# Where a graph-transformer layer fills a scratch tensor, and which engines take a maximum over partitions

## The reference, cut to what matters

```
xn = layernorm(x)
x  = x + gnn(xn, edges) + mix(xn)          # mix: attention with random features, 16 heads of 64
x  = x + ffn(layernorm(x))                 # 8 experts, the two best of each row, softmax of their logits
# gnn: h = xn @ W.T + b; out = segment_sum(deg^-1/2[row] * deg^-1/2[col] * h[col], row)
# mix: q, k, v = xn @ W.T + b; phi = exp(x @ orf.T - |x|^2/2) + eps; out = phi(q) @ (phi(k).T @ v) / (phi(q) @ sum phi(k))
# ffn: out = sum over the two experts e of score_e * (x @ expert_w[e] + expert_b[e])
```

## Time and profile before

| | value |
|---|---|
| median of three runs | 1686.0 us |
| profiled execution, its own time | 1684.43 us |
| its span, first to last instruction | 1682.3 us |
| mean granted TensorE clock, share of full | 0.954 |
| TensorE matmul / VectorE / ScalarE / GpSimd busy | 88% / 44% / 26% / 20% |
| DMA traffic over the span | 150.64 MB |

### The profile page before, as it was taken

One profiled execution on the slowest core, in us unless ns is written; L12 is line 12 of the kernel. 1 busy time (PEld: TensorE's weight loads), 2 busy tenths in 40 slices (PEclk: granted clock), 3 DMA queues, 4 the chain that ended last, 5 costly groups with the idle time before them and its releaser, 6 DMA issues.

```text
span 1682.3 us, 25130 instructions
## 1 busy us (share of the span) xinstructions
PE 1477.8 (88%) x7987; PEld 1219.1 (72%) x8051; DVE 747.2 (44%) x1413; ACT 436.9 (26%) x727; POOL 343.4 (20%) x333
## 2 busy tenths in 40 slices
PE   4718788899998999999999999998999589999990
PEld 1406667664446999999999999997788578888870
DVE  6805555412002454544544444444545514554436
ACT  6300111111001333332333232333213202332320
POOL 5510212112310111010110101000413311212233
PEclk9959999999999999999999999999999679999995
DMA  3580001141211000000000000000432515566648
GB/s 144 190 287 10 22 5 35 35 144 63 94 63 35 26 23 19 21 25 12 25 12 25 25 12 25 0 1 19 127 125 95 200 56 206 194 237 246 234 167 298
DMA packets 54830, 150.64 MB, mean 90 GB/s; under 512 B 7130, under 2 KB 14250, under 8 KB 54480
## 3 DMA queue, kind: packets, MB, share of 16 engines
q1 hardware_dynamic: 48096, 127.20, 21.5%
q0 software_dynamic: 6688, 22.83, 4.3%
HBM read 119.72 MB, written 48.64 MB: 100 GB/s over the span
## 4 chain that ended last, share of the span: by engine, by line
PE 82%; DVE 5%; issue 4%; another core or an unknown queue 2%; DMA 2%; ACT 2%; POOL 2%; DVEq 1%; POOLq 0%; SPq 0%; ACTq 0%
PE PB L1406 10%; PE PB L1435 7%; PE PB L1437 7%; PE PB L1436 7%; PE PB L1611 5%; PE PB L1612 5%; PE PB L1614 5%; PE PB L1471 4%; PE PB L1494 4%; PE PB L1356 4%; PE PB L1394 2%; PE PB L1417 2%; PE PB L1395 2%; PE PB L1396 2%
## 5 line engine op out<-in xcount | busy, mean ns | idle before, releaser
L1435 PE MATMUL PB<-xh,hw 128*128 128x416 f32 (+1 forms) x576 | 206.0, 358 | 4.9 <-POOL orfl L692 4.9
L1437 PE MATMUL PB<-xh,hw 128*128 128x416 f32 (+1 forms) x576 | 204.1, 354 | 0.0
L1436 PE MATMUL PB<-xl,hw 128*128 128x416 f32 (+1 forms) x576 | 203.9, 354 | 0.0
L1406 PE MATMUL PB<-h,AT 128*128 128x512 f32 x400 | 171.9, 592 | 1.2 <-ACT h L835 1.2
L1611 PE MATMUL PB<-mwh,mth 128*128 128x512 f32 x368 | 149.0, 405 | 1.3 <-issue 1.3
L1406 PEld LDWEIGHTS PB<-h,AT 128*128 128x128 f32 x400 | 75.9, 190 | 96.5 <-issue 94.6
L1612 PE MATMUL PB<-mwl,mth 128*128 128x512 f32 x368 | 144.6, 393 | 0.0
L1356 PE MATMUL PB<-ohs,ohd 128*128 x471 | 103.6, 342 | 42.4 <-DVE ohs L1031 29.1
L1394 PE MATMUL PB<-wqh,xh 128*128 128x256 f32 x320 | 93.5, 292 | 41.6 <-ACT h L829 39.9
L1029 DVE TENSOR_SCALAR ohd<-iota,dc 128x128 f16 x178 | 69.1, 388 | 134.0 <-PE PB L1356 122.3
L658 POOL CAST hw<-hraw 128x1024 fp32r<-128x1024 f32 x24 | 24.9, 1038 | 477.8 <-PE PB L1437 469.5
(11 more groups left out here) (230 smaller groups left out, 2837.6 us busy)
## 6 DMA issues: line engine op xcount, KB each, us to landing
mraw<-expert_w SPq DMA_DIRECT2D x64, 512.0 KB, 5.4
slot_y<-ybuf SPq DMA_DIRECT2D x46, 256.0 KB, 3.4
xrow<-x SPq DMA_DIRECT2D x20, 256.0 KB, 2.7
y_scratch<-xrow SPq DMA_DIRECT2D x20, 256.0 KB, 2.0
yrow<-y_scratch SPq DMA_DIRECT2D x20, 256.0 KB, 2.8
x2n_half<-xhat SPq DMA_DIRECT2D x20, 256.0 KB, 2.5
out<-x SPq DMA_DIRECT2D x9, 512.0 KB
AT<-wg SPq DMA_DIRECT2D x32, 128.0 KB, 2.2
```

Source lines behind the costliest of these rows:

```text
L1406: ins = mm(bank(4 + u % 2), AT[:, b, t * P:(t + 1) * P], hh[c][:, b, :], start=(b == 0), stop=(b == TT - 1))
L1435: mm(bank(i, n), hw[:, wi, 0, k, :], xh[:, k, c0:c0 + n], start=(k == 0), stop=False)
L1436: mm(bank(i, n), hw[:, wi, 0, k, :], xl[:, k, c0:c0 + n], start=False, stop=False)
L1437: ins = mm(bank(i, n), hw[:, wi, 1, k, :], xh[:, k, c0:c0 + n], start=False, stop=(k == KT - 1))
```

## The change

Two independent edits. First, the four fill DMAs leave the loop over slabs of `W`. In their place each of the seven rounds of SP's loop over head pairs issues one of `FILL` = 640 rows, behind the round's three weight loads; the wait before the experts counts seven. Second, the maximum over partitions is no longer an instruction of GpSimd: TensorE transposes `ext` into PSUM bank 6 (20 partitions, 80 columns), VectorE takes the maximum along the row into `extm` (20 x 1), and a TensorE matmul with the identity turns that into one row of 20 in bank 7, which VectorE reads where it read `extr`.

```diff
+FILL = MAXT * P // (KT - 1)
+assert FILL * (KT - 1) == MAXT * P and FILL <= NP
...
@@ sync @@
             for i in range(NQ * KT):
                 q, k = i // KT, i % KT
-                if i == KT:
-
-                    for r0 in range(0, MAXT * P, NP):
-                        n = min(NP, MAXT * P - r0)
-                        sp.dma_start(slot_y[r0:r0 + n, :], x[0:n, :]).then_inc(slots_filled, 16)
                 if i >= 4:
                     sp.wait_ge(w_ready, i - 3)
...
                     sp.wait_ge(a_w, START + 3 * j + i)
                     sp.dma_start(hraw[:, :, :], w[ds(j, 1)].rearrange("a p k n -> (a p) k n")).then_inc(a_raw, 16)
+                sp.dma_start(slot_y[ds((j - 1) * FILL, FILL), :], x[0:FILL, :]).then_inc(slots_filled, 16)
...
-            sp.wait_ge(slots_filled, 16 * -(-MAXT * P // NP))
+            sp.wait_ge(slots_filled, 16 * (KT - 1))
@@ gpsimd @@
-            pool.wait_ge(s_ext, 1)
-            g.partition_all_reduce(extr[:, :], ext[:, :], PAIRS, RMAX).then_inc(s_extr, 1)
@@ vector @@
             dve.wait_ge(s_extr, 1)
+            v.tensor_reduce(extm[:, :], PB[0:2 * TT, 512 * 6:512 * 6 + PAIRS], AX.X, ALU.max).then_inc(s_extm, 1)
+            dve.wait_ge(s_extr, 2)
+            extr = bank(7, 2 * TT)
             link(v.tensor_scalar(rng[:, 0, :], extr[0:1, TT:2 * TT], -1.0, float(PAIRS), ALU.mult, ALU.add))
@@ tensor @@
+            pe.wait_ge(s_cst2, 9)
+            pe.wait_ge(s_ext, 1)
+            nc.tensor.transpose(PB[0:2 * TT, 512 * 6:512 * 6 + PAIRS], ext[:, :], ident[0:PAIRS, 0:PAIRS]).then_inc(s_extr, 1)
+            pe.wait_ge(s_extm, 1)
+            mm(PB[0:1, 512 * 7:512 * 7 + 2 * TT], extm[:, :], ident[0:2 * TT, 0:2 * TT], start=True, stop=True).then_inc(s_extr, 1)
             pe.wait_ge(s_rng, 1)
-            pe.wait_ge(s_cst2, 9)
```

More of the change, by code:

```diff
@@ L50 @@
 ds = bass.ds
-RMAX = bass.bass_isa.ReduceOp.max
 def gps_layer(nc, x, dst_pairs, src_cols, dst_cols, wg, bg, wq, bq, wk, bk, wv, bv, wo, bo, orf,
@@ L140, in gps_layer @@
         ext = keep("ext", [PAIRS, 2 * TT], F32, pb)
-        extr = keep("extr", [PAIRS, 2 * TT], F32, pb)
+        extm = keep("extm", [2 * TT, 1], F32, pb)
         rng = keep("rng", [1, 4, TT], F32, pb)
@@ L254, in gps_layer @@
         s_extr = sem("s_extr")
+        s_extm = sem("s_extm")
         s_rng = sem("s_rng")
```

## The result

The changed kernel takes 1640.64 us (median of 4 runs, 1637.92 to 1642.52) against 1686.76 us of the kernel before, run in turn (4 runs). The ratio is 0.9723, 95% interval 0.9702 to 0.9745. That is 46 us less; forecast were 47.6, and 1638 us. A later set on another chip gave 1640.05 and a ratio of 0.9734 (0.9719 to 0.9748). The profiled execution took 1637.92 us, span 1636.1.

A forecast was written before the change was run, and what follows sets the result against it. The prediction took TensorE to bound the kernel, busy 88% of the span, with a long wait before tile 2. Its terms, 37.95 + 2.37 + 7.3 + 0 = 47.6 us, gave 1638 us, range 1632 to 1648.

The forecast's parts named there:

- three signs of being wrong: TensorE waits in front of tile 2, block 0 ends later than 61.5, or a head pair takes longer than before.
- Term 1: Fill leaves the slabs of W, so TensorE's wait before tile 2 goes: 37.95 us, between 36.5 and 37.95.
- Term 2: Without the wait, tile 2 on TensorE keeps the upper clock level: 2.37 us, between 2.0 and 3.0.
- Term 3: Maximum over partitions leaves GpSimd, before block 0: 7.3 us, between 5.9 and 7.7, lower bound 4.6 with slower fetching.
- I count nothing: In block 0, GpSimd's work beside VectorE's one-hots slows them equally in either position, so zero.
- the fallback: GpSimd's first normalization stays at 23.82, block 0 isn't taken out before 63.3: Term 3 shrinks to 4.8 us, 1641; 9%.
- Term 4: Fills in the loop over head pairs cost zero, with a bound of 0.5 us a round, 3.5 us in all.
- slower than before: Rival: in the head-pair loop a load sticks behind each fill and TensorE waits, costing 58 us, giving 1696; 1%.

The follow-up runs named there:

- e1: Kernel before with only the fill moved into the loop over head pairs, the reduction left on GpSimd: 1645.59 us, ratio 0.9764.
- e4: Changed kernel with 16 matmuls of 128 x 512 on zeros put between tile 2 and block 1: 1637.83 us.
- e12: Changed kernel as it is, run again beside other experiments on the same chip: 1640.05 us, ratio 0.9734 to the kernel before.
- e3: Changed kernel with the reduction put back on GpSimd at its old place, its result unused: 1640.01 us, ratio 0.9736.
- e10: Changed kernel with eight ring slabs for W, edge-column conversions behind the ranges, GpSimd's quarter 0 low parts after block 0: 1632.32 us, ratio 0.9694.
- e6: Changed kernel with four times the fill in each round, the extra three going to a spare tensor: 1641.10 us, ratio 0.9748.
- e5: Changed kernel with each round's fill put ahead of the load of wv instead of behind wq: 1641.35 us, ratio 0.9751.
- e13: The kernel of e3 again, beside the changed kernel on the same chip: 1641.89 us, ratio 0.9747.
- e7: Changed kernel with GpSimd's low parts of quarters 2 and 3 one addition to the degrees earlier; no time given, block 6 took 10.25 us instead of 9.00.
- e9: Changed kernel with the order of e7 and VectorE's two edge-column conversions moved behind the ranges: 1639.33 us, ratio 0.9732.

## Why the prediction was right

Of its three signs of being wrong none showed: tile 2 has no wait, block 0 ends at 60.40, and a head pair takes 79.9 to 80.1 us as before.

**Term 1, the wait: right, to the hundredth.** Tile 2 gained 45.67 - 7.72 = 37.95 us over tile 0. Its basis was to copy the sequence that followed the wait, 6.29 us, to the place where the wait had begun, and to see that it still ends before TensorE asks (0.58 us to spare by the sum, 0.66 in the trace: tile 0 is taken out at 79.71). e1 shows it alone.

**Term 2, the clock: mis-sized.** Tile 2 itself gained 48.00 - 45.67 = 2.33 us, as said. But block 1 took 18.69 us after and 17.61 before, and 1.08 us of it went back: while the matmuls of tile 2 ran at 1.2 GHz the sequencer got ahead, and block 1's first rounds had no bubble (e4's reading of it). The term is 1.25 us. I had written that only that tile gains since the clock was back; right about the clock, and silent on what half-speed work had paid for. I had also written that the clock needn't fall in a wait of a microsecond or two: it didn't in the changed kernel's first profile, and it did in e12's, in a wait of 1.67 us.

**Term 3, the maximum: right, a little small.** 8.20 us at the ranges for the 7.3 forecast, outside my bounds of 5.9 to 7.7: the new route took 1.01 us, below my bound of 1.2, since the allowance of 0.4 for first instructions was not needed, and 0.28 us came from `ext`, complete at 7.22 instead of 7.50. What was removed isn't a fixed price either: 8.93 us in the profile I forecast from, 7.63 in e1. "I count nothing" for GpSimd beside the one-hots was off: from the ranges to the end of block 0, 8.20 became 7.73. e3 and e10 show that the subtractions lengthen the block where they meet it, by 2 to 3 us; before and after they met it alike (47.99 and 48.46 us), so "equally" was nearly right. That GpSimd would start its normalizations at 9.2 was read correctly out of two gaps, and e3 shows the delay that the fallback named (block 0 is taken out at 63.37 instead of 60.65). The Trainium skill's advice to leave a reduction over partitions to GpSimd (GPSIMD Engine Reference, Engine selection) is not borne out at 80 x 20: 1.01 us against 8.93 on the path, or 7.63 in e1.

**Term 4, the fills: right at zero, for a reason weaker than the true one.** They land in 11.0 to 12.5 us, not in 8.3, and the rounds keep their length. My bound, that a fill must be over before the next load, was far too tight: in e6 the fills overrun it and TensorE waits for nothing, and in e5 the load is late to GpSimd itself and a round is longer by 0.2 us at most. The rival "slower than before" had its price on the wrong engine.

**The sum.** The profiled executions differ by 46.5 us (1684.43 to 1637.92): 47.6, less the 1.1 of block 1, plus 0.9 at the ranges, less 0.5 in block 0, less some 0.4 net in later stages. So the closeness is partly luck: the misses of terms 2 and 3 nearly cancel. The later stages hold luck too. In quarter 2 the changed kernel's profile kept its clock and that of the kernel before did not, 0.9 us in its favour by the end of block 4, and the end of the kernel took 1.1 us longer than before, within its scatter. The median lies 2.6 us above the forecast. One part is block 1. A second, by the profile of e12, is the clock in the short waits of 1.7 to 2 us, worth 1.5 us at tile 0 and 0.5 to 0.9 in quarter 2: both were kept at 2.4 GHz in the profiled execution and neither in e12's. How often each happens in unprofiled runs can't be read.

## What to carry to other kernels

A bulk transfer that nobody needs soon belongs in a queue's idle stretch, and its price where it stands is not its own length but how long the first small load behind it keeps an engine waiting. Price a late load by the engine at the end of the line: a helper that waits for the load may have a buffer's depth to give away. When two edits meet in the same wait their gains overlap, so measure each alone before adding them up.

## What the runs showed of the hardware

- One `partition_all_reduce` of 80 x 20 keeps GpSimd from everything else for about 16 us at the kernel's start (before, e3, e13); the trace shows 0.43 to 0.59 us as busy and names ScalarE for part of the rest. Its result came 8.93 us after its operand in one profile and 7.63 in another.
- GpSimd's subtractions slow VectorE's one-hots beside them: 128 x 1280 takes 1.06 us instead of 0.54, while a fill at 300 GB/s alone leaves it at 0.54.
- A loop of six matmuls of 1.30 us takes 1.71 us a round, with the operands ready. After 16 matmuls of 512 columns, or 24 at 1.2 GHz, three rounds pass without the bubble, worth 0.8 to 1.1 us, as if the sequencer had got ahead; block 4 shows the same behind tiles at the lower clock.
- A wait of 1.67 us in front of tile 0 left the clock at 2.4 GHz in 11 profiles and halved it in three (e7, e10, e12).
- In one head pair of e9 the clock sagged (mean 0.66 from 840 to 850 us, the round took 82.6 us instead of 80.0), and the wait in front of the matmuls was no longer than at the same place in the changed kernel (0.52 us in e9, 0.51 there). I have no cause for it.
